# Thirteen filler matmuls ahead of the first products, the first attention's front ordered by batch half, and a comparison as a two-operand operation

## The chip, the cores and the metric

The kernel runs on one core of a Trainium2 chip. A core has TensorE (matmuls; PE in the profile, with PEld for its weight loads), VectorE (DVE), ScalarE (ACT), GpSimd (POOL) and SyncE (SP, which only issues transfers here). The metric is the device time of one execution in microseconds, as the median of several runs; lower is better.

## The reference

The kernel computes four layers on x, of 2 batches x 256 tokens x 128 features, all in float32, and each adds to x behind a scalar gate:

```python
x = x + tanh(g_xattn[0]) * L0_xattn(layernorm(x), ctx)    # 16 heads of 8; head h attends only to keys h, h+16, ...
x = x + tanh(g_ffn[0]) * L0_ffn(layernorm(x))             # 8 experts, each takes the 64 tokens with its best scores
x = x + tanh(g_xattn[1]) * L1_xattn(layernorm(x), ctx, ctx)  # 16 heads over all 512 context rows
x = x + tanh(g_ffn[1]) * L1_ffn(layernorm(x))             # 16 experts, one per token, plus a shared one
```

The change touches the first layer and one step of the second. In the first, a head sees one key in sixteen, so that the scores of all heads fit into one product of a token tile with the keys, if the keys are masked so that row d of key s is kept only where feature d belongs to head s mod 16:

```python
Q = (hidden @ Wq.T + bq);  K = (ctx @ Wk.T + bk);  V = (ctx @ Wv.T + bv)
attn = softmax(Q_h @ K_h[h::16].T * 8 ** -0.5);  out = (attn @ V_h[h::16]) @ Wo.T + bo
```

## The kernel before

The 512 tokens are four tiles of 128 (`NT`), two for each batch; the context is 2 x 512 rows, a half for each batch. Everything stays in SBUF, and PSUM is one tensor `bank` of eight banks. Each engine has its program written out by hand, and the engines meet only in semaphores: `then_inc` on the instruction that makes something, `wait_ge` ahead of the one that needs it. Nothing is reordered by a planner, so what is queued behind a waiting instruction waits too.

Transfers: SP issues x, the two halves of the context (`ctx`, `ctx_b`), constants and the later weights (lines 318 to 330). ScalarE's queue brings the identity and masks (`const`) and the weights `w0`, GpSimd's queue the small vectors (`small`), gates and rows.

The front of the first attention, by engine:

- VectorE takes statistics of the four x tiles (`ln_stats`), normalises them (`ln_apply`, line 1139, a tensor-scalar operation from SBUF to SBUF, 128 columns), copies the ones column of the values (`va0`, line 1150), masks the two halves of the keys from PSUM into `k0` (line 1155), and makes two broadcast columns `bvcol` (line 1162, two copies from SBUF to SBUF). Then come the four softmax tiles: a maximum (line 1175) and a subtraction (line 1176) each; `masked_v` (line 1168) takes the values of a half out of PSUM behind the third and the fourth.
- GpSimd computes the inverse deviations (lines 367, 371). Then it waits for the first masked keys, `k0_sb`, and fills three areas, one after the other, each awaited before the next: `va1` with zeros (4096 columns, line 395), its ones column (line 397), and the lower half of `kpack` with zeros (8192 columns, line 399). Behind these stand the gated bias and the residual tiles `xb`.
- TensorE transposes normalised tiles 0 and 1, multiplies the first context half into keys (`keys0`, lines 492 to 493), transposes tiles 2 and 3, and goes on to `queries0`, `keys0(1)`, `scores0`. It then waits for `bvcol_set` and for rows, adds the bias row, makes the value products (eight, bank 2 and 3), and goes on to the turned probabilities and the weighted sums `weighted0`.
- ScalarE copies the four turned tiles (line 978), then makes four query tiles `q0T` (line 984), then the exponentials.

A float32 product stands in the trace as two records, each a pass of its own.

In the second layer VectorE finds the 64th best score of each expert (`edge`), and compares all scores with it: `atleast` (line 1223, a tensor-scalar operation with `edge` as its scalar, 16 partitions x 256), and `gradeT` (line 1224, with two tensors). Meanwhile TensorE runs value products of the second attention, then `keep_running(28, 7)`, 28 products of zeros that nobody reads (line 602), and then transposes `gradeT`. `zeros_bf`, set by GpSimd, is the stationary operand of all such fillers.

Of the kernel before, what the change touches and what calls it, by code (L numbers as in the profile page):

```python
# [25 lines left out]
P = 128  # L26
D = 128
NB = 2
SQ = 256
SK = 512  # L30
T = NB * SQ
NT = T // P
KC = SK // P
H = 16
DH = D // H
# [9 lines left out]
HE = 2 * E0  # L45
HT = T // 2
# [26 lines left out]
V_BQ, V_BK, V_BV, V_LNW, V_LNB, V_BQ1, V_BK1, V_BV1 = range(8)  # L73
# [25 lines left out]
ALU = mybir.AluOpType  # L99
ACT = mybir.ActivationFunctionType  # L100
AX_X = mybir.AxisListType.X
F32 = mybir.dt.float32
BF16 = mybir.dt.bfloat16
# [3 lines left out]
def build(nc, x, small, consts, selq, onerows, gates, rows, ctxT, w0, w1, fc1T, fc2, b2, shGU, shD, gateup, down, kscr, qscr, out):  # L107
    with ExitStack() as ctx:
        def sb(name, shape, dt=F32):
            return ctx.enter_context(nc.sbuf_tensor(name, shape, dt))  # L110
# [4 lines left out]
        bank = ctx.enter_context(nc.psum_tensor("bank", [P, 8, 512], F32))  # L115
# [21 lines left out]
        def vec(n):  # L137
            return small_sb[:, C_VEC + n:C_VEC + n + 1]
# [19 lines left out]
        normedT = [sb(f"normedT{k}", [P, NT, P]) for k in range(2)] * 2  # L158
# [8 lines left out]
        selq_bf = sb("selq_bf", [P, 3, HPE, NROW], BF16)  # L167
        selq_up = sb("selq_up", [P, 3, HPE, NROW], BF16)
        iota_bf = sb("iota_bf", [P, CAP0], BF16)
        zeros_bf = sb("zeros_bf", [P, P], BF16)  # L170
        bvcol = sb("bvcol", [P, 2, P])
        bias = sb("bias", [P, 2, D])
        gbias = sb("gbias", [P, 2, D])
# [8 lines left out]
        def late_view(at, n, pattern, dt=F32, **k):  # L182
# [100 lines left out]
                                           "b2", "sh", "gu", "down")}  # L283

        S = {n: sem(n) for n in (
            "half_set", "vchain", "gchain", "tanh_done", "consts_bf", "bvcol_set", "k0_ps", "v0_ps", "k0_sb",
            "va0_sb", "bias0_ps", "bias0_sb", "xb0", "xb1", "nT0_ps", "nT0_sb", "q0_ps", "q0_sb", "sc0_ps",
            "shift0", "probs0_sb", "p0T_ps", "p0T_sb", "pv0_ps", "att0", "attT0_ps", "attT0_sb", "o0_ps", "nT1_ps",
            "nT1_sb", "lg0_ps", "sh0", "ex0", "score_sb", "scT_ps", "top_zero", "gradeT_sb", "grade_ps", "above_sb", "equal_sb",
# [64 lines left out]
        def _(pool):  # L354
# [1 line left out]
            pool.dma_start(gates_sb[:], gates).then_inc(L["gates"], 16)  # L356
            pool.dma_start(rows_sb[:], rows).then_inc(L["rows"], 16)
            pool.dma_start(b2_sb[:], b2).then_inc(L["b2"], 16)
            pool.memset(minus_half[:], -0.5).then_inc(S["half_set"], 1)
            pool.memset(zeros_bf[:], 0.0).then_inc(S["half_set"], 1)  # L360
            pool.memset(top[:], 0.0).then_inc(S["top_zero"], 1)
            pool.wait_ge(S["half_set"], 1)

            def ln_rstd(k, i):

# [4 lines left out]
                pool.wait_ge(S["gchain"], gc[0])  # L370
                pool.tensor_tensor(rstd[:, k, i:i + 2], rstd[:, k, i:i + 2], minus_half[:, i:i + 2], ALU.pow)\  # L371
                    .then_inc(LN_RS, 2)

            gc = [0]

            def link(ins):

                gc[0] += 1
                ins.then_inc(S["gchain"], 1)
                pool.wait_ge(S["gchain"], gc[0])  # L380

            def residual_bias(l, src):

# [91 lines left out]
        def _(pe):  # L475
            def mm(o, lhsT, rhs, start=True, stop=True, **k):
                return pe.matmul(o, lhsT, rhs, start=start, stop=stop, **k)  # L477
# [5 lines left out]
            def keep_running(n, at_bank):  # L483

                for _ in range(n):
                    mm(bank[:, at_bank, 0:T], zeros_bf[:], selq_bf[:].rearrange("p k h r -> p (k h r)")[:, 0:T])

            def normed0_turned(i):
                pe.wait_ge(LN_N, 0 * NT + i + 1)
# [2 lines left out]
            def keys0(b):  # L492
                mm(bank[:, b, :], w0_sb[:, 1, :], ctxT_sb[:, b * SK:(b + 1) * SK]).then_inc(S["k0_ps"], 1)

            def queries0(i):
                pe.wait_ge(S["nT0_sb"], i + 1)
                if i >= 2:
                    pe.wait_ge(S["q0_sb"], i - 1)
                mm(bank[:, 2 + i % 2, 0:P], w0_sb[:, 0, :], normedT[0][:, i, :]).then_inc(S["q0_ps"], 1)

            def scores0(i):
                pe.wait_ge(S["k0_sb"], i // 2 + 1)
                pe.wait_ge(S["q0_sb"], i + 1)
                mm(bank[:, 4 + i, :], q0T[:, i, :], k0[:, i // 2, :]).then_inc(S["sc0_ps"], 1)

            pe.wait_ge(L["const"], 16)
            normed0_turned(0)
            normed0_turned(1)
            pe.wait_ge(L["w0"], 16)
            pe.wait_ge(L["ctx"], 16)  # L510
            keys0(0)
            normed0_turned(2)
            normed0_turned(3)
            queries0(0)
            queries0(1)
            pe.wait_ge(L["ctx_b"], 16)
            keys0(1)
            scores0(0)
            scores0(1)
            queries0(2)  # L520
            queries0(3)
            scores0(2)
# [75 lines left out]
            mm(bank[:, 6, 0:D], bvcol[:, 1, :], w1_sb[:, 3, :], stop=False)  # L598
            mm(bank[:, 6, 0:D], const_sb[0:1, K_ONE:K_ONE + P], rows_sb[0:1, 1, :], start=False).then_inc(S["bias1_ps"], 1)
            pe.wait_ge(L["selq"], 16)  # L600
            pe.wait_ge(S["half_set"], 2)
            keep_running(28, 7)
            pe.wait_ge(S["gradeT_sb"], 1)
            pe.wait_ge(S["bias1_sb"], 1)
# [256 lines left out]
            def no_window(at_bank):  # L861

                for w, n in ((0, T), (1, WIDE - T)):
                    mm(bank[:, at_bank + w, 0:n], zeros_bf[:], selq_bf[:].rearrange("p k h r -> p (k h r)")[:, 0:n])

            def gate_up(e, at):
                for k, o in ((0, gate_ps), (1, up_ps)):
# [100 lines left out]
        def _(act):  # L968
# [5 lines left out]
            def copies(ps, sbs, dst, src):  # L974

                for i in range(NT):
                    act.wait_ge(S[ps], i + 1)
                    act.copy(dst(i), src(i)).then_inc(S[sbs], 1)  # L978

            act.wait_ge(L["small"], 16)  # L980
            copies("nT0_ps", "nT0_sb", lambda i: normedT[0][:, i, :], lambda i: bank[:, 4 + i, 0:P])
            for i in range(NT):
                act.wait_ge(S["q0_ps"], i + 1)
                act.activation(q0T[:, i, :], bank[:, 2 + i % 2, 0:P], ACT.Identity, bias=vec(V_BQ)).then_inc(S["q0_sb"], 1)
            for i in range(NT):
                act.wait_ge(S["shift0"], i + 1)
                act.activation(probs0[:, i, :], shifted[:, i, :], ACT.Exp, scale=SCALE).then_inc(S["probs0_sb"], 1)
# [136 lines left out]
        def _(dve):  # L1124
            chain = [0]

            def link(ins):

                chain[0] += 1
                ins.then_inc(S["vchain"], 1)  # L1130
                dve.wait_ge(S["vchain"], chain[0])
# [5 lines left out]
            def ln_apply(k, i):  # L1137
                dve.wait_ge(LN_RS, ln_done(k, i))
                dve.tensor_scalar(normed[k][:, i, :], ln_in[k][:, i, :], meanvar[:, k, i, 0:1], rstd[:, k, i:i + 1],  # L1139
                                  ALU.subtract, ALU.mult).then_inc(LN_N, 1)  # L1140

            dve.wait_ge(L["x"], 16)
            for i in range(NT):
                ln_stats(0, i, x_sb[:, i, :])
            for i in range(NT):
                ln_apply(0, i)
            dve.wait_ge(L["const"], 16)
            he = const_sb[:, K_HE:K_HE + H]
            hs = const_sb[:, K_HS:K_HS + H]
            dve.tensor_copy(va0[:, :, :, DH:DH + 1],  # L1150
                            hs.unsqueeze(1).unsqueeze(3).to_broadcast([P, NB * KC, H, 1]))
            dve.wait_ge(L["small"], 16)
            for b in range(NB):
                dve.wait_ge(S["k0_ps"], b + 1)
                dve.scalar_tensor_tensor(
                    out=k0[:, b, :].rearrange("p (j h) -> p j h", h=H),
                    in0=bank[:, b, :].rearrange("p (j h) -> p j h", h=H), scalar=vec(V_BK),
                    in1=he.unsqueeze(1).to_broadcast([P, SK // H, H]), op0=ALU.add, op1=ALU.mult)\
                    .then_inc(S["k0_sb"], 1)

            for l, v in ((0, V_BV), (1, V_BV1)):
                dve.tensor_copy(bvcol[:, l, :], vec(v).to_broadcast([P, P])).then_inc(S["bvcol_set"], 1)

# [56 lines left out]
            link(dve.stream_shuffle(other[:], top[:], [(p + E0) % HE if p < HE else p for p in range(32)]))  # L1220
            link(dve.tensor_tensor(pairmax[:], top[0:HE, :], other[0:HE, ::-1], ALU.max))
            link(dve.tensor_reduce(edge[:], pairmax[:], AX_X, ALU.min))
            link(dve.tensor_scalar(atleast[:], scoreT, edge[:], None, ALU.is_ge))
            dve.scalar_tensor_tensor(out=gradeT[:], in0=scoreT, scalar=edge[:], in1=atleast[:],
                                     op0=ALU.is_gt, op1=ALU.add).then_inc(S["gradeT_sb"], 1)
            dve.wait_ge(S["grade_ps"], 1)
# [292 lines left out]
```

## Time and profile before

| | before |
|---|---|
| median of 3 runs | 185.77 us (185.43 to 186.42) |
| the profiled execution's own time | 186.36 us |
| its span, first to last instruction | 184.5 us |
| mean granted clock of TensorE | 0.972 |
| busy: PE / DVE / ACT / POOL | 87% / 60% / 47% / 34% |

Busy shares are averages over stages. The page also follows the chain of work that ended last back from the last instruction. Where two steps of a helper share a line (477 and 481 are the matmul and the transpose of every stage), the tile names tell them apart: `w_sb` is `w0_sb` or `w1_sb`, `va` is `va0` or `va1`, `k` and `bvcol` are as in the code. A timeline row gives start, length, engine, line, operation, tiles and count; where operations of a row follow each other closely they are merged (x2, x4). A bracket tells how long the engine sat idle before, and who ended that. A row of a window (`39.50:40.00`) gives its length, then the busy time of PE, PEld, DVE, ACT and POOL, and last the granted clock as a share of full speed, the DMA share and GB/s.

### The profile page before, as it was taken

Reading aid. Unit: us, or ns where it says so; the run is one execution under the profiler, and the core shown is the slowest. Engines: PE = TensorE matmul, PEld = TensorE weight load, DVE = VectorE, ACT = ScalarE, POOL = GpSimd, SP = SyncE. Lnnn points to the kernel's source line nnn. Section 1 sums busy time; section 2 is a strip of 40 time slices with the busy share of each in tenths; the row PEclk is TensorE's granted clock in tenths of the full one; section 3 lists DMA queues with packets and bytes.
Section 4 is the critical chain, followed back from the end, with each engine's and each line's share of the span. In section 5 each row is a group of like instructions: output and inputs, shape, how many; then the busy total and the mean of one; then the engine's idle time right before and its main releaser. Section 6 shows DMA issues by size and latency. Waiting matters only on the chain.

```text
span 184.5 us, 3393 instructions
## 1 busy us (share of the span) xinstructions
PE 159.9 (87%) x1260; PEld 107.0 (58%) x1260; DVE 109.8 (60%) x300; ACT 85.9 (47%) x148; POOL 61.8 (34%) x91
## 2 busy tenths in 40 slices
PE   0599997699999999988999999989965876899994
PEld 0356883564589884754454444435434634499994
DVE  1557767796733475899988988970514695001032
ACT  2124537252046106548987787788820454301020
POOL 6489904986192722697000000000203342000000
PEclk9999999569999999999999999999999789999999
DMA  5999800005777590005200000000015000000002
GB/s 163 382 350 430 367 13 2 0 18 154 171 160 149 108 362 25 25 23 89 39 4 0 0 4 0 0 4 0 0 21 210 0 2 2 4 0 4 0 0 64
DMA packets 4294, 15.43 MB, mean 84 GB/s; under 512 B 948, under 2 KB 1844, under 8 KB 3492
## 3 DMA queue, kind: packets, MB, share of 16 engines
q1 hardware_dynamic: 2980, 11.66, 20.2%
q10 hardware_dynamic: 576, 2.44, 4.0%
q0 software_dynamic: 720, 1.09, 2.8%
q8 instruction: 12, 0.20, 0.4%
q14 instruction: 6, 0.05, 0.1%
HBM read 13.94 MB, written 1.25 MB: 82 GB/s over the span
## 4 chain that ended last, share of the span: by engine, by line
PE 74%; DVE 14%; issue 5%; POOL 2%; ACT 2%; DMA 2%; POOLq 0%
PE bank L477 69%; DVE mx L1326 6%; PE bank L481 5%; DVE stats L1134 2%; DMA x_sb<-in_x 2%; POOL rstd L371 2%; DVE normed L1139 1%; DVE meanvar L1135 1%; DVE res_b L1190 1%; POOL rstd L367 1%; PE bank L650 0%; ACT outT L1061 0%; DVE res_b L1292 0%; DVE kpack L1369 0%; ACT va L1100 0%
## 5 line engine op out<-in xcount | busy, mean ns | idle before, releaser
L1326 DVE TENSOR_REDUCE mx<-bank 128x1 f32<-128x512 f32 x64 | 41.7, 687 | 5.0 <-PE bank L477 4.5
L1067 ACT ACTIVATE arena<-bank 128x1024 f32<-128x1024 f32 x32 | 31.9, 1025 | 8.3 <-PE bank L477 7.8
L367 POOL TENSOR_SCALAR rstd<-meanvar 128x2 f32<-128x2 f32 x10 | 2.2, 223 | 65.4 <-DVE meanvar L1135 65.4
L477 PE MATMUL bank<-kpack,fc1T_sb 72*128 72x512 bf16 x64 | 22.7, 383 | 0.7 <-DVE mx L1326 0.5
L477 PE MATMUL bank<-fc1T_sb,kpack 104*128 104x256 bf16 x128 | 19.3, 272 | 0.1
L477 PE MATMUL bank<-arena,va 128*32 128x256 f32 x256 | 18.6, 387 | 0.5 <-ACT outT L1061 0.5
L477 PEld LDWEIGHTS bank<-fc1T_sb,kpack 104*128 104x128 bf16 x128 | 12.0, 97 | 6.4 <-issue 1.6
L477 PE MATMUL bank<-selq_bf,zeros_bf 128*128 128x512 bf16 (+1 forms) x57 | 13.4, 379 | 1.4 <-issue 1.4
L481 PE MATMUL bank<-const_sb,normed 128*128 128x128 f32 x16 | 4.5, 347 | 9.7 <-DVE normed L1139 9.5
L477 PEld LDWEIGHTS bank<-kpack,fc1T_sb 72*128 72x128 bf16 x64 | 6.1, 97 | 11.3 <-issue 5.2
L481 PEld LDWEIGHTS bank<-const_sb,normed 128*128 128x128 f32 x16 | 2.3, 156 | 14.1 <-issue 7.1
L477 PE MATMUL bank<-normedT,shGU_sb 128*128 128x256 f32 (+1 forms) x24 | 9.3, 536 | 1.3 <-issue 1.3
L477 PEld LDWEIGHTS bank<-arena,va 128*32 128x32 f32 x256 | 6.2, 108 | 6.8 <-issue 4.6
L477 PEld LDWEIGHTS bank<-selq_bf,zeros_bf 128*128 128x128 bf16 x57 | 5.5, 100 | 7.0 <-issue 2.1
L477 PE MATMUL bank<-kpack,arena 128*128 128x128 f32 (+1 forms) x72 | 8.6, 278 | 0.0
L1408 DVE TENSOR_TENSOR kpack<-bank,kpack 128x768 f32<-128x768 f32 x1 | 1.0, 957 | 12.7 <-ACT kpack L1115 12.7
L1075 ACT CAST fc1T_sb<-bank 8x1024 bf16<-8x1024 f32 x8 | 8.0, 1005 | 0.9 <-PE bank L477 0.8
L477 PEld LDWEIGHTS bank<-kpack,arena 128*128 128x128 f32 x72 | 8.2, 192 | 0.3 <-issue 0.2
L477 PE MATMUL bank<-kpack,fc_sb 128*128 x64 | 7.4, 276 | 1.0 <-ACT kpack L1113 1.0
L477 PEld LDWEIGHTS bank<-kpack,fc_sb 128*128 128x128 f32 x64 | 7.2, 192 | 1.2 <-issue 1.2
L978 ACT COPY normedT<-bank 128x128 f32<-128x128 f32 x12 | 2.9, 266 | 10.4 <-PE bank L481 10.3
L371 POOL TENSOR_TENSOR rstd<-rstd,minus_half 128x2 f32<-128x2 f32 x10 | 7.1, 713 | 1.5
(223 smaller groups left out, 314.8 us busy)
## 6 DMA issues: line engine op xcount, KB each, us to landing
kpack<-k_parts SPq DMA_DIRECT2D x3, 768.0 KB
fc1T_sb<-in_fc1T SPq DMA_DIRECT2D x1, 2048.0 KB, 11.8
fc_sb<-in_fc SPq DMA_DIRECT2D x1, 2048.0 KB, 16.1
fc_sb<-in_gateup ACTq DMA_DIRECT2D x2, 1024.0 KB, 6.0
arena<-in_down SPq DMA_DIRECT2D x1, 1024.0 KB, 6.4
k_parts<-arena SPq DMA_DIRECT2D x8, 96.0 KB, 2.2
fc1T_sb<-q_rows POOLq DMA_DIRECT2D x9, 64.0 KB, 2.8
ctxT_sb<-in_ctxT SPq DMA_DIRECT2D x2, 256.0 KB, 4.7
```

The lines of the kernel that those rows point to most:

```text
L367: pool.tensor_scalar(rstd[:, k, i:i + 2].unsqueeze(2), meanvar[:, k, i:i + 2, 1:2], EPS, None, ALU.add)\
L371: pool.tensor_tensor(rstd[:, k, i:i + 2], rstd[:, k, i:i + 2], minus_half[:, i:i + 2], ALU.pow)\
L477: return pe.matmul(o, lhsT, rhs, start=start, stop=stop, **k)
L481: return pe.transpose(o, src, ident[0:n, 0:n])
L978: act.copy(dst(i), src(i)).then_inc(S[sbs], 1)
L1067: act.activation(probs1[:, n % (2 * GH), :, :], bank[:, 2 + 2 * (n % 2):4 + 2 * (n % 2), :], ACT.Exp, scale=SCALE)\
L1075: act.copy(qpack[MROW:KROWS, b, g * GH:(g + 1) * GH, :], bank[MROW:KROWS, r, 0:SQ].unsqueeze(1).to_broadcast([2 * GH, GH, SQ]))\
L1134: link(dve.bn_stats(stats[:, k, i, :], src))
L1135: dve.bn_aggr(meanvar[:, k, i, :], stats[:, k, i, :]).then_inc(LN_MV, 1)
L1139: dve.tensor_scalar(normed[k][:, i, :], ln_in[k][:, i, :], meanvar[:, k, i, 0:1], rstd[:, k, i:i + 1], ALU.subtract, ALU.mult).then_inc(LN ...
L1190: dve.scalar_tensor_tensor(out=res[0][:, i, :], in0=bank[:, 4 + i, 0:D], scalar=tanhg[:, 0:1], in1=xb_sb[:, i, :], op0=ALU.mult, op1=ALU.a ...
L1326: dve.tensor_reduce(mx1[:, b * 2 + qt, g * GH + j:g * GH + j + 1], bank[:, r, :], AX_X, ALU.max)\
```

## The change

Three edits.

*Fillers.* VectorE first sets a new tile `quiet` (128 x 512, bfloat16) to zero, ahead of its wait for x, and `zeros_bf` becomes its first 128 columns. TensorE waits for that alone and issues 13 products of 512 columns out of `quiet` into bank 7, which nobody reads, before its first wait for data. GpSimd's memset of `zeros_bf` and the semaphore `half_set`, and TensorE's wait on it ahead of the 28 fillers, are gone; GpSimd's `link` helper is defined earlier and now orders the memset of `minus_half`.

*Order by halves.* TensorE, ScalarE and VectorE now do everything of batch half 0 (tiles 0 and 1, context half 0) as far as the scores before half 1. On TensorE the first keys product stands ahead of the transposes and ahead of the wait for `const`. On VectorE the masking of the first keys stands between the normalisations of tiles 0, 1 and those of tiles 2, 3, and the `va0` copy behind those. The `bvcol` copies stay behind the masking of the second keys.

*Comparison.* `atleast` becomes a tensor-tensor operation, with `edge` broadcast along the row as its second operand.

```diff
-        zeros_bf = sb("zeros_bf", [P, P], BF16)
+        quiet = sb("quiet", [P, T], BF16)
+        zeros_bf = quiet[:, 0:P]
@@ gpsimd
-            pool.memset(minus_half[:], -0.5).then_inc(S["half_set"], 1)
-            pool.memset(zeros_bf[:], 0.0).then_inc(S["half_set"], 1)
+            link(pool.memset(minus_half[:], -0.5))
             pool.memset(top[:], 0.0).then_inc(S["top_zero"], 1)
-            pool.wait_ge(S["half_set"], 1)
@@ tensor
+            pe.wait_ge(S["quiet_set"], 1)
+            for _ in range(13):
+                mm(bank[:, 7, 0:T], zeros_bf, quiet[:])
+            pe.wait_ge(L["w0"], 16)
+            pe.wait_ge(L["ctx"], 16)
+            keys0(0)
             pe.wait_ge(L["const"], 16)
             normed0_turned(0)
             normed0_turned(1)
-            pe.wait_ge(L["w0"], 16)
-            pe.wait_ge(L["ctx"], 16)
-            keys0(0)
+            queries0(0)
+            queries0(1)
+            scores0(0)
+            scores0(1)
+            pe.wait_ge(L["ctx_b"], 16)
+            keys0(1)
             normed0_turned(2)
             normed0_turned(3)
-            queries0(0)
-            queries0(1)
-            pe.wait_ge(L["ctx_b"], 16)
-            keys0(1)
-            scores0(0)
-            scores0(1)
             queries0(2)
             queries0(3)
...
-            pe.wait_ge(S["half_set"], 2)
             keep_running(28, 7)
@@ scalar
-            copies("nT0_ps", "nT0_sb", lambda i: normedT[0][:, i, :], lambda i: bank[:, 4 + i, 0:P])
-            for i in range(NT):
-                act.wait_ge(S["q0_ps"], i + 1)
-                act.activation(q0T[:, i, :], bank[:, 2 + i % 2, 0:P], ACT.Identity, bias=vec(V_BQ)).then_inc(S["q0_sb"], 1)
+            for half in ((0, 1), (2, 3)):
+                for i in half:
+                    act.wait_ge(S["nT0_ps"], i + 1)
+                    act.copy(normedT[0][:, i, :], bank[:, 4 + i, 0:P]).then_inc(S["nT0_sb"], 1)
+                for i in half:
+                    act.wait_ge(S["q0_ps"], i + 1)
+                    act.activation(q0T[:, i, :], bank[:, 2 + i % 2, 0:P], ACT.Identity, bias=vec(V_BQ)).then_inc(S["q0_sb"], 1)
@@ vector
+            dve.memset(quiet[:], 0.0).then_inc(S["quiet_set"], 1)
             dve.wait_ge(L["x"], 16)
             for i in range(NT):
                 ln_stats(0, i, x_sb[:, i, :])
-            for i in range(NT):
-                ln_apply(0, i)
-            dve.wait_ge(L["const"], 16)
...
+            for i in (0, 1):
+                ln_apply(0, i)
+            dve.wait_ge(L["const"], 16)
+            dve.wait_ge(L["small"], 16)
+            masked_keys(0)
+            for i in (2, 3):
+                ln_apply(0, i)
+            dve.tensor_copy(va0[:, :, :, DH:DH + 1],
+                            hs.unsqueeze(1).unsqueeze(3).to_broadcast([P, NB * KC, H, 1]))
+            masked_keys(1)
             for l, v in ((0, V_BV), (1, V_BV1)):
                 dve.tensor_copy(bvcol[:, l, :], vec(v).to_broadcast([P, P])).then_inc(S["bvcol_set"], 1)
...
-            link(dve.tensor_scalar(atleast[:], scoreT, edge[:], None, ALU.is_ge))
+            link(dve.tensor_tensor(atleast[:], scoreT, edge[:].to_broadcast([HE, HT]), ALU.is_ge))
```

## Rows read from the trace of the kernel before

**Rows 1.** The page: granted clock in 40 slices, and the chain by engine.
```profile
PEclk9999999569999999999999999999999789999999
...
PE 74%; DVE 14%; issue 5%; POOL 2%; ACT 2%; DMA 2%; POOLq 0%
```

**Rows 2.** Timeline of 0 to 30 us, all engines: start, length, engine, line.
```profile
0.73 0.39 SPq L318 DMA_DIRECT2D x_sb<-in_x  x1
...
6.49 0.66 PE L481 MATMUL bank<-const_sb,normed 128*128 128x128 f32 x2 [6.49 <-DVE normed L1139]
...
7.58 0.28 DVE L1150 COPY va<-const_sb 128x128 f32<-128x128 f32 x1
...
9.78 3.51 POOL L395 MEMSET va<- 128x4096 f32 x1 [2.75 <-DVE k L1155]
...
11.88 0.75 DVE L1155 SCALAR_TENSOR_TENSOR k<-bank,small_sb,const_sb 128x512 f32<-128x512 f32 x1 [2.16 <-PE bank L477]
...
13.36 0.67 DVE L1175 TENSOR_REDUCE mx<-bank 128x16 f32<-128x512 f32 x1
...
13.74 6.92 POOL L399 MEMSET kpack<- 64x8192 f32 x1
...
17.26 2.05 PE L477 MATMUL bank<-w_sb,ctxT_sb 128*128 128x128 f32 x16
...
18.46 0.88 DVE L1168 TENSOR_TENSOR va<-bank,const_sb 128x128 f32<-128x128 f32 x4 [1.06 <-PE bank L477]
...
20.43 1.25 PE L477 MATMUL bank<-va,arena 128*128 128x144 f32 x8 [0.24 <-ACT arena L993]
```

**Rows 3.** Passes of the score products: count, ns min/median/max, first and last start.
```profile
L477 PE MATMUL bank<-k,q0T x8: 592/592/1051, 11.6 to 16.1; 128*128 128x512 f32 x8
```

**Rows 4.** Timeline of VectorE in short windows: normalisations, then each bvcol copy.
```profile
5.99 0.61 DVE L1139 TENSOR_SCALAR normed<-x_sb,meanvar,rstd 128x128 f32<-128x128 f32 x2 [0.54 <-POOL rstd L371]
...
12.55 0.82 DVE L1162 COPY bvcol<-small_sb 128x128 f32<-128x128 f32 x1
...
12.68 0.76 DVE L1162 COPY bvcol<-small_sb 128x128 f32<-128x128 f32 x1
```

**Rows 5.** Timelines of GpSimd and VectorE, and line 1391 (ns min/median/max).
```profile
43.18 1.06 DVE L1223 TENSOR_SCALAR atleast<-q0T,edge 16x256 f32<-16x256 f32 x1
...
142.12 0.67 POOL L460 IOTA kpack<- 128x640 f32 x1
...
142.20 0.74 DVE L1139 TENSOR_SCALAR normed<-res_b,meanvar,rstd 128x128 f32<-128x128 f32 x2 [1.20 <-POOL rstd L371]
...
142.74 0.34 POOL L462 MEMSET kpack<- 128x128 f32 x1
...
150.10 1.40 POOL L469 TENSOR_TENSOR va<-va 128x512 f32<-128x512 f32 x1 [1.82 <-ACT va L1103]
...
152.23 1.15 POOL L471 TENSOR_TENSOR va<-va 128x512 bf16<-128x512 f32 x1 [0.73 <-ACT va L1106]
...
L1391 DVE TENSOR_SCALAR kpack<-kpack,place x4: 544/548/1447, 149.0 to 150.4; 128x640 bf16<-128x640 f32 x4
```

**Rows 6.** TensorE and VectorE near the 28 fillers; clock of one half microsecond.
```profile
34.59 3.62 PE L477 MATMUL bank<-w_sb,ctxT_sb 128*128 128x128 f32 x16
...
39.29 0.86 PE L477 MATMUL bank<-selq_bf,zeros_bf 128*128 128x512 bf16 x2
...
39.50:40.00 0.50, 0.50 (x3) 0.16 (x2) 0.47 (x3) 0.16 (x1) 0.50 (x2) 0.65 0.00 0
...
44.28 0.47 DVE L1224 SCALAR_TENSOR_TENSOR gradeT<-q0T,edge,atleast 16x256 f32<-16x256 f32 x1
...
45.69 0.29 PE L481 MATMUL bank<-const_sb,gradeT 16*128 16x16 f32 x2
```

**Rows 7.** Transfers: size and median us from issue to landing (issued at 1.18 and 1.64).
```profile
ctxT_sb<-in_ctxT SPq DMA_DIRECT2D x2, 256.0 KB, 4.7
```

More of the change, by code:

```diff
@@ L285, in build @@
         S = {n: sem(n) for n in (
-            "half_set", "vchain", "gchain", "tanh_done", "consts_bf", "bvcol_set", "k0_ps", "v0_ps", "k0_sb",
+            "quiet_set", "vchain", "gchain", "tanh_done", "consts_bf", "bvcol_set", "k0_ps", "v0_ps", "k0_sb",
             "va0_sb", "bias0_ps", "bias0_sb", "xb0", "xb1", "nT0_ps", "nT0_sb", "q0_ps", "q0_sb", "sc0_ps",
@@ L358, in _, with link @@
             pool.dma_start(b2_sb[:], b2).then_inc(L["b2"], 16)
-            pool.memset(minus_half[:], -0.5).then_inc(S["half_set"], 1)
-            pool.memset(zeros_bf[:], 0.0).then_inc(S["half_set"], 1)
+            gc = [0]
+            def link(ins):
+                gc[0] += 1
+                ins.then_inc(S["gchain"], 1)
+                pool.wait_ge(S["gchain"], gc[0])
+            link(pool.memset(minus_half[:], -0.5))
             pool.memset(top[:], 0.0).then_inc(S["top_zero"], 1)
-            pool.wait_ge(S["half_set"], 1)
             def ln_rstd(k, i):
@@ L372, in ln_rstd @@
                     .then_inc(LN_RS, 2)
[L374 to L380, printed above, removed]
             def residual_bias(l, src):
@@ L485, in keep_running @@
                 for _ in range(n):
-                    mm(bank[:, at_bank, 0:T], zeros_bf[:], selq_bf[:].rearrange("p k h r -> p (k h r)")[:, 0:T])
+                    mm(bank[:, at_bank, 0:T], zeros_bf, selq_bf[:].rearrange("p k h r -> p (k h r)")[:, 0:T])
             def normed0_turned(i):
@@ L863, in no_window @@
                 for w, n in ((0, T), (1, WIDE - T)):
-                    mm(bank[:, at_bank + w, 0:n], zeros_bf[:], selq_bf[:].rearrange("p k h r -> p (k h r)")[:, 0:n])
+                    mm(bank[:, at_bank + w, 0:n], zeros_bf, selq_bf[:].rearrange("p k h r -> p (k h r)")[:, 0:n])
             def gate_up(e, at):
@@ L1144, in _, with masked_keys @@
                 ln_stats(0, i, x_sb[:, i, :])
-            for i in range(NT):
-                ln_apply(0, i)
-            dve.wait_ge(L["const"], 16)
             he = const_sb[:, K_HE:K_HE + H]
             hs = const_sb[:, K_HS:K_HS + H]
[L1150 to L1153, printed above, removed]
+            def masked_keys(b):
                 dve.wait_ge(S["k0_ps"], b + 1)
```

## Prediction, made before the changed kernel was run

> **What bounds the kernel now.** I read the page first, for its chain of work [rows 1]: TensorE carries 74% of it, but that is an average, and what an edit is worth has to be read from its own stage. So the next view is the timeline of the first 28 us [rows 2]. TensorE begins at 6.49 us. It is busy from there, yet slow: one pass of a 128x512 f32 product takes 1.05 us up to about 12.5 and 0.59 us afterwards [rows 3], which are the two levels of its clock, 1.2 and 2.4 GHz. (The page's granted clock says full speed in both places [rows 1]; only the durations show it here.) From 13.36 VectorE works through the softmax tiles, each a maximum (0.67 us) and a subtraction, and from 20.43 TensorE runs nearly back to back through the weighted sums. Behind 20.43 all follows in a fixed order, so what the front gains or loses up to the first weighted sum passes on to the end, apart from what the clock does further down.
>
> The second thing to see is what holds VectorE at 12.55. The two bvcol copies take 0.82 and 0.76 us and end at 13.37 and 13.44 [rows 4], though a copy of the same 128x128 size takes 0.28 [rows 2]. GpSimd's memset of va1 runs from 9.78 to 13.29 [rows 2]; both copies end right behind it. Two more places look alike [rows 5]. The pair of normalisations at 142.20 takes 0.74 us, not 0.61 as at 5.99 [rows 4], and ends just behind GpSimd's iota (142.12 + 0.67). The last selection of line 1391 takes 1.45 us against 0.55 for the least of the four, and ends 0.35 us behind GpSimd's subtraction (150.10 + 1.40). So copies and tensor-scalar operations from SBUF to SBUF, normalisations among them, are held while GpSimd works on a large tile. Operations that read PSUM are not: masking the second half of the keys took 0.75 us at 11.88, in the middle of the memset [rows 2].
>
> **The change part by part.** *Fillers.* VectorE can set quiet from 0.73 us, when the queues start [rows 2]. The nearest rows for the memset are the 0.28 us copy and the 0.67 us maximum over 512 columns [rows 2]; I take 0.45, so that fillers start at about 1.2. One costs 0.43 us at the low clock (two run in 0.86 [rows 6]) and half of that at the high one. Thirteen end at 6.8 if all are slow, at 4.0 if all are fast. The first context half and w0 land about 1.18 + 4.7 = 5.9 [rows 7], so the first keys product, which now waits for nothing else, runs between 5.9 and 6.8: the fillers cost at most 0.9 us of readiness. The clock rose 6.0 us (6.49 to 12.5) and 5.3 us (34.59 to 39.85, where the granted clock of the half microsecond is 0.65) after dense work began [rows 3, 6]; from 1.2 on that is 6.5 to 7.2, so keys run fast or nearly so.
>
> *Front by halves.* Keys take two passes, 0.43 + 0.59 = 1.02 us fast, their masking 0.75. Masking of half 0 ended just before 9.78, where it released the memset of va1. Now it ends at T0 = 7.7 to 8.6, say 8.2 (9.5 if keys are still slow), and releases that memset at once. But two normalisations now stand right behind this masking on VectorE; before, they were over when the va0 copy began at 7.58. VectorE starts an operation 0.08 us before the last one ends (bvcol at 12.55, masking until 12.63), and the second of a pair 0.26 us after the first (0.61 - 0.35). So they start at T0-0.08 and T0+0.18, and the second at least meets the memset and waits for its end, E = T0 + 3.6 = 11.8. That GpSimd gets in between two queued VectorE operations is what line 1391 shows: its subtraction, issued at 150.10 during one selection, took 0.25 us more than the like one at 152.23, and then held the next selection [rows 5].
>
> Queued behind on VectorE: the va0 copy (0.28, until 12.1), the masking of half 1 (0.75, until 12.8; its keys are there at 11.6: q0T at 8.9, two score products of 0.85, keys 1.02), then, from 12.7, the bvcol copies. GpSimd goes on meanwhile: its kpack memset starts 0.45 us behind the end of va1's (13.74 after 13.29), at 12.25, for 6.92 us. Before, bvcol slipped in between the two; now it comes half a microsecond too late and is held until 12.25 + 6.92 = 19.2, done at 19.3 against 13.44. Behind bvcol stand all four softmax tiles on VectorE, and on TensorE, which waits for bvcol_set, the bias row and the value products.
>
> To the first weighted sum two paths compete. VectorE: three tiles take 4.04 us (13.36 to 17.40, where its idle 1.06 us before 18.46 begin), masking of V 0.88 [rows 2]: 19.2 + 4.04 + 0.88 = 24.1, that is 3.7 us later than 20.43, the least loss. TensorE: bias 0.73 and values 2.05 us fast, 1.4 and 3.6 slow [rows 2, 6]; then 1.2 us (from 17.26 + 2.0 to 20.43) for transposes and their copy, up to 1.7 slow. It has been idle since about 15 by then. All slow, 19.3 + 1.4 + 3.6 + 1.7 = 26.0, a loss of 5.6. I take 4.9, nearer the slow end: after the thin stretch before 34.59 the clock was low, but a pause of four microseconds need not do it. T0 moves this by 0.4 either way.
>
> *Other waits.* On ScalarE the copies of tiles 2 and 3 now stand behind q0T of half 0; those tiles come from the late normalisations anyway. kpack's memset ends 1.5 us earlier than before (19.2, 20.66), so GpSimd's xb tiles and SP's transfer of ones behind kpack_zero come no later. The memset of zeros_bf and the waits on half_set that go stood in stretches where GpSimd waited for statistics and TensorE ran fillers: nothing.
>
> *Comparison.* With two operands it costs 0.47 us by the nearest row (line 1224, the same tile, two SBUF inputs [rows 6]) and at most the present 1.06 if it is held [rows 5]: 0 to 0.6 us of VectorE. But gradeT is ready at 44.28 + 0.47 = 44.75 and the transposes that use it start at 45.69, behind the 28 fillers [rows 6]. With that cover of 0.94 us it is worth nothing. Had the value products of 34.59 run at the high clock (2.05 instead of 3.6 us), VectorE would be last and the edit would count in full.
> The Trainium skill ("SBUF — State Buffer", Who interferes with whom) says that a VectorE operation with two SBUF inputs contends with a GpSimd one that reads SBUF; by it the new form would be held at line 1223 like the old and give nothing even then, so that the chance kept below for it would go. No row here shows that form beside a large GpSimd operation.
>
> **The sum.** Against the profiled execution (span 184.5, time 186.36 us): +4.9, so 191.3. That execution lies 0.6 us above the median of 185.77, so the median goes to 190.7. This case alone reaches from 189.0 (3.7 less 0.4) to 191.8 (5.6 plus 0.4).
>
> **Rivals.** *A, the pair gets through (the other side).* VectorE keeps its turn over both normalisations. For it: the held pair at 142.20 was out by 142.94 though GpSimd's next memset had been issued at 142.74 [rows 5]; against it, line 1391. The memset of va1 then runs from T0+0.5 to 12.1, kpack's from 12.6. Masking of half 1 ends at 12.4, and bvcol, issued at 12.3, goes first. First maximum at 12.8 (0.6 earlier), the second half's scores done at 14.9 instead of 16.7, values at 17.6 (19.3), first weighted sum at 18.8: 1.6 us gained, between 1.1 and 2.4. Median 184.1. It decides from where bvcol is issued before kpack's memset, and it has 0.3 us for that.
> The same section of the skill has the ports given to one side for a whole instruction, to whoever issues first; by that rule the turn isn't kept over a pair and A falls, which gives 190.7. The row at 142.20 doesn't decide it, since the memset behind it is short.
>
> *B, only the normalisation is held.* bvcol still comes ahead of kpack's memset, because GpSimd needs 0.5 us longer between its memsets than the 0.45 of [rows 2]. First maximum at 13.2, values at 17.8: 1.4 us gained, 184.4.
>
> *C, the front doesn't count.* Nothing is held and the clock further down takes the gain back: within 0.9 us of now. The stage from 20.43 on has no slack that speaks for it.
>
> **How the numbers follow.** Forecast, bvcol held by kpack's memset: 0.63. A 0.22, B 0.11 (in a few hundredths of these the comparison counts too), C 0.04. A measurement of this kernel tells 0.5%, 0.93 us, from no change. So faster 0.33, same 0.04, slower 0.63. The forecast is the likeliest case, 190.7, with its own 189.0 to 191.8. As a third of the chance lies on the other side, the range goes from 183.4 (A less 0.7) to 191.8.
>
> **What would show it.** Right: the bvcol copies last some 6 us and end within 0.2 us of kpack's memset; a normalisation of tile 2 or 3 lasts about 3.5 us; the first maximum is past 18.5. Wrong: normalisations of 0.35 us beside the memset, or bvcol done before 13.5. Fillers: thirteen, ending by 6.8, and keys at 0.59 us a pass. Comparison: gradeT earlier, its transposes behind the fillers as late as before.

## The result

The changed kernel takes 191.5 us (median of 4 runs, 191.29 to 191.72), the kernel before in the same comparison 185.6 us (184.38 to 186.42). The ratio is 1.0333, with a 95% interval of 1.0292 to 1.0374. The case of the forecast (bvcol held by the memset of kpack) came true. Its 190.7 us was 0.8 us too low, near the upper end of its own range (191.8).

| | before | after |
|---|---|---|
| profiled execution: time, span | 186.36, 184.5 us | 191.72, 189.9 us |
| mean granted clock | 0.972 | 0.955 |
| first maximum on VectorE | 13.36 us | 19.07 us |
| first weighted sum on TensorE | 20.43 us | 25.71 us |
| from there to the end of the span | 164.1 us | 164.2 us |

The page of the changed kernel, the lines that answer to [rows 1]: a dip has come into the granted clock in the fourth and fifth slice of 4.7 us (8, then 5), and in the chain that ended last `bvcol` is new, with 3%, and `normed` has gone from 1% to 3%. VectorE made both late.

```profile
PEclk9998599957999999999999999999999879999999
...
PE 69%; DVE 20%; issue 5%; DMA 3%; POOL 2%; ACT 1%; ACTq 0%; POOLq 0%; DVEq 0%
PE bank L476 64%; DVE mx L1337 6%; PE bank L480 4%; DVE bvcol L1173 3%; DVE normed L1143 3%; DMA w_sb<-in_w 3%; DVE stats L1138 2%; POOL rstd L378 1%; DVE meanvar L1139 1%; DVE res_b L1201 1%; DVE k L1156 1%; PE bank L651 0%; ACT outT L1065 0%; POOL rstd L374 0%; DVE res_b L1303 0%
```

The timeline of the changed kernel from 0 to 26 us, all engines (columns as in [rows 2]):

```profile
0.85 0.27 DVE L1146 MEMSET quiet<- 128x256 uint32 x1 [0.85 <-PEq L1518]
...
1.18 4.44 PE L476 MATMUL bank<-quiet 128*128 128x512 bf16 x13 [1.18 <-DVE quiet L1146]
...
5.98 1.12 PE L476 MATMUL bank<-ctxT_sb,w_sb 128*128 128x512 f32 x2 [0.37 <-DMA w_sb<-in_w]
...
7.25 0.75 DVE L1156 SCALAR_TENSOR_TENSOR k<-bank,small_sb,const_sb 128x512 f32<-128x512 f32 x1 [0.40 <-PE bank L476]
...
7.92 3.80 DVE L1143 TENSOR_SCALAR normed<-x_sb,meanvar,rstd 128x128 f32<-128x128 f32 x2
8.06 3.51 POOL L394 MEMSET va<- 128x4096 f32 x1 [0.78 <-DVE k L1156]
...
11.64 0.49 DVE L1169 COPY va<-const_sb 128x128 f32<-128x128 f32 x1
...
11.77 0.74 DVE L1156 SCALAR_TENSOR_TENSOR k<-bank,small_sb,const_sb 128x512 f32<-128x512 f32 x1
12.05 6.95 POOL L398 MEMSET kpack<- 64x8192 f32 x1
...
12.43 6.71 DVE L1173 COPY bvcol<-small_sb 128x128 f32<-128x128 f32 x2
...
19.07 0.67 DVE L1186 TENSOR_REDUCE mx<-bank 128x16 f32<-128x512 f32 x1
...
19.20 0.80 PE L476 MATMUL bank<-w_sb,bvcol 128*128 128x128 f32 x2 [3.82 <-DVE bvcol L1173]
...
20.65 3.78 PE L476 MATMUL bank<-w_sb,ctxT_sb 128*128 128x128 f32 x16
...
23.03 0.87 DVE L1179 TENSOR_TENSOR va<-bank,const_sb 128x128 f32<-128x128 f32 x4
...
25.71 0.51 PE L476 MATMUL bank<-va,arena 128*128 128x144 f32 x2 [0.24 <-ACT arena L997]
```

Read it from the memsets. The one of `va1` ends at 11.57; the pair of normalisations that began at 7.92 ends at 11.72. The one of `kpack` ends at 19.00, the pair of `bvcol` copies at 19.14. In between GpSimd began `kpack` at 12.05 and VectorE came to `bvcol` at 12.43, 0.38 us too late. TensorE sat idle for 3.82 us, for `bvcol` alone. The windows around that idle time (length, busy PE, PEld, DVE, ACT, POOL, granted clock, DMA share, GB/s) show the granted clock fall to half in it (0.82, then 0.50), and rise again in the half microsecond from 24.50, more than 5 us after work resumed at 19.20. So the value products ran at 1.2 GHz (3.78 us; 2.05 in [rows 2]):

```profile
17.50:18.00 0.50, 0.00 (x0) 0.00 (x0) 0.50 (x2) 0.00 (x0) 0.50 (x1) 0.82 0.85 360
18.00:18.50 0.50, 0.00 (x0) 0.00 (x0) 0.50 (x2) 0.00 (x0) 0.50 (x1) 0.50 1.00 426
24.00:24.50 0.50, 0.50 (x5) 0.50 (x4) 0.50 (x1) 0.00 (x0) 0.00 (x0) 0.50 0.00 0
24.50:25.00 0.50, 0.50 (x6) 0.50 (x5) 0.47 (x1) 0.00 (x0) 0.00 (x0) 0.85 0.00 0
```

The second place, the comparison (timeline of 34 to 52 us), answers to [rows 5, 6]. The new form takes 1.19 us beside GpSimd's subtraction, and the transposes of `gradeT` still stand behind the fillers, 0.81 us after it is ready at 50.17.

```profile
44.98 6.07 PE L476 MATMUL bank<-selq_bf,quiet 128*128 128x512 bf16 x27 [0.33 <-issue]
...
48.23 1.16 POOL L420 TENSOR_TENSOR arena<-arena 128x512 f32<-128x512 f32 x1 [0.73 <-ACT arena L1029]
48.48 1.19 DVE L1234 TENSOR_TENSOR atleast<-q0T,edge 16x256 f32<-16x256 f32 x1
...
49.70 0.47 DVE L1235 SCALAR_TENSOR_TENSOR gradeT<-q0T,edge,atleast 16x256 f32<-16x256 f32 x1
...
50.98 0.29 PE L480 MATMUL bank<-const_sb,gradeT 16*128 16x16 f32 x2
```

Some executions take over 1.5% longer than the fastest of their kernel: in the table below, medians are over all executions, ratios leave such ones out, and the profiled execution of e1 was one of them (187.78 us), so that its rest is not given.

### The profile page after: what moved, and what is told of

Read it like the earlier page. It is cut to its first block, busy times and chain, and to the rows that moved or that the text cites. A ratio compares the mean times of both kernels' runs of the same rounds, so it can differ in the third digit from the quotient of the medians.

```text
span 189.9 us, 3412 instructions
## 1 busy us (share of the span) xinstructions
PE 164.5 (87%) x1268; PEld 109.4 (58%) x1273; DVE 118.9 (63%) x301; ACT 85.8 (45%) x148; POOL 61.8 (33%) x90
## 4 chain that ended last, share of the span: by engine, by line
PE 69%; DVE 20%; issue 5%; DMA 3%; POOL 2%; ACT 1%; ACTq 0%; POOLq 0%; DVEq 0%
PE bank L476 64%; DVE mx L1337 6%; PE bank L480 4%; DVE bvcol L1173 3%; DVE normed L1143 3%; DMA w_sb<-in_w 3%; DVE stats L1138 2%; POOL rstd L378 1%; DVE meanvar L1139 1%; DVE res_b L1201 1%; DVE k L1156 1%; PE bank L651 0%; ACT outT L1065 0%; POOL rstd L374 0%; DVE res_b L1303 0%
## 5 line engine op out<-in xcount | busy, mean ns | idle before, releaser
L476 PE MATMUL bank<-fc1T_sb,kpack 104*128 104x256 bf16 x128 | 19.3, 272 | 0.1
L476 PE MATMUL bank<-selq_bf,quiet 128*128 128x512 bf16 (+1 forms) x52 | 12.1, 374 | 2.3 <-issue 2.1
L476 PEld LDWEIGHTS bank<-selq_bf,quiet 128*128 128x128 bf16 x57 | 5.5, 100 | 7.2 <-issue 2.2
L476 PEld LDWEIGHTS bank<-normedT,shGU_sb 128*128 128x128 f32 x24 | 5.3, 237 | 3.8 <-issue 3.1
L476 PE MATMUL bank<-w_sb,ctxT_sb 128*128 128x128 f32 x32 | 7.4, 426 | 0.0
L476 PE MATMUL bank<-arena,fc1T_sb 128*128 128x64 f32 x64 | 7.3, 275 | 0.0
```

## The experiments

All are given in one table. "Rest" is the span of the profiled execution less the start of its first weighted sum. Kernels of a group ran together with the kernel before, whose median there stands behind the group's name. Its executions spread over some 4 us (183.97 to 187.96), so differences below half a per cent are not read.

| kernel | first maximum | first weighted sum | rest | median (n) | ratio to before, 95% |
|---|---|---|---|---|---|
| before / after | 13.36 / 19.07 | 20.43 / 25.71 | 164.1 / 164.2 | 185.6 / 191.5 (4) | 1.0333 [1.0292, 1.0374] |
| *group 1 (before: 185.53)* | | | | | |
| e1_pool_behind_bvcol | 13.02 | 19.23 | | 185.18 (12) | 0.9981 [0.9934, 1.0028] |
| e2_bvcol_first | 12.37 | 18.95 | 163.6 | 184.58 (10) | 0.9977 [0.9939, 1.0015] |
| e3_bvcol_up_pool_behind | 12.08 | 18.55 | 163.9 | 184.37 (10) | 0.9974 [0.9939, 1.0010] |
| e6_kpack_in_two | 16.36 | 21.34 | 163.5 | 186.67 (4) | 1.0115 [1.0056, 1.0173] |
| *group 2 (before: 184.96)* | | | | | |
| e10_bvcol_two_operands | 12.91 | 19.19 | 163.9 | 184.92 (10) | 1.0002 [0.9972, 1.0032] |
| e4_fillers_alone | 12.63 | 17.82 | 164.1 | 182.99 (4) | 0.9877 [0.9822, 0.9932] |
| e5_order_no_fillers | 14.86 | 21.34 | 163.9 | 187.27 (10) | 1.0052 [0.9999, 1.0105] |
| e8_old_comparison | 12.51 | 18.99 | 163.3 | 184.14 (12) | 0.9957 [0.9926, 0.9988] |
| *group 3 (before: 186.06)* | | | | | |
| e11_fillers_bvcol_first | 10.43 | 17.71 | 163.8 | 183.29 (4) | 0.9844 [0.9793, 0.9896] |
| e12_keys_ahead_too | 10.82 | 18.09 | 164.3 | 183.48 (4) | 0.9851 [0.9797, 0.9906] |
| e7_cmp_alone | 13.42 | 20.46 | 164.3 | 185.92 (12) | 0.9996 [0.9961, 1.0031] |

The rest is 163.3 to 164.3 us in all these traces: the first weighted sum tells the time of a profiled execution to within a microsecond.

### Is it the hold of bvcol, and what decides it?

**e1**: GpSimd starts its memsets behind `bvcol` instead of behind the first masked keys.

```diff
-            pool.wait_ge(S["k0_sb"], 1)
+            pool.wait_ge(S["bvcol_set"], 2)
```

> The changed kernel, with one wait replaced: GpSimd begins its three memsets behind bvcol_set (2) instead of behind the first masked keys. Theory H (a copy or normalisation of VectorE from SBUF to SBUF is held while GpSimd fills a large tile, and the bvcol copies are what costs): nothing is held, bvcol is done at 12.6, the first maximum starts at 12.5 (19.07 in the changed kernel), the first weighted sum at 18.6 (25.71), and the time falls by about 7 us to 184.4. The residual tiles of GpSimd may then be late by a few tenths. Rival R (the order by halves or the clock costs by itself, the long copies only stand beside it): the copies may be short, but the time stays above 190.

Nothing is held, and the first weighted sum comes 6.5 us earlier than in the changed kernel. The memsets themselves now begin at 13.16:

```profile
8.48 0.59 DVE L1143 TENSOR_SCALAR normed<-x_sb,meanvar,rstd 128x128 f32<-128x128 f32 x2
...
12.75 0.35 DVE L1173 COPY bvcol<-small_sb 128x128 f32<-128x128 f32 x2
...
13.16 3.51 POOL L394 MEMSET va<- 128x4096 f32 x1 [6.17 <-DVE bvcol L1173]
```

**e2**: the changed kernel with the two copies ahead of the first masking.

```diff
+            for l, v in ((0, V_BV), (1, V_BV1)):
+                dve.tensor_copy(bvcol[:, l, :], vec(v).to_broadcast([P, P])).then_inc(S["bvcol_set"], 1)
             masked_keys(0)
...
             masked_keys(1)
-            for l, v in ((0, V_BV), (1, V_BV1)):
-                dve.tensor_copy(bvcol[:, l, :], vec(v).to_broadcast([P, P])).then_inc(S["bvcol_set"], 1)
```

> The changed kernel, with the bvcol copies moved ahead of the masking of the first keys; GpSimd as it was. H: the copies take 0.3 us; the normalisations of tiles 2 and 3 are still held for 3.6 us by the memset of va1, but they cost little, since the second keys are ready only at 11.5; first maximum at 12.5, first weighted sum at 18.8, 184.5 us. If the held normalisations are a large part of the loss instead, the time stays 2 us or more above the kernel with GpSimd moved. R: above 190.

The copies are free; the normalisations are held as before, and that costs next to nothing:

```profile
6.70 0.35 DVE L1167 COPY bvcol<-small_sb 128x128 f32<-128x128 f32 x2
...
7.75 3.80 DVE L1143 TENSOR_SCALAR normed<-x_sb,meanvar,rstd 128x128 f32<-128x128 f32 x2
...
7.90 3.51 POOL L394 MEMSET va<- 128x4096 f32 x1 [0.68 <-DVE k L1156]
...
11.54 0.44 PE L480 MATMUL bank<-const_sb,normed 128*128 128x128 f32 x2
```

The transposes of tiles 2 and 3, which need these normalisations, start at 11.54 and have no bracket, so TensorE did not sit idle before them: in this order it is at the second keys until then.

**e3**: GpSimd waits as in e1, and the copies stand right behind the normalisations of tiles 2 and 3.

> The changed kernel, with the bvcol copies right behind the normalisations of tiles 2 and 3, and GpSimd's memsets behind bvcol_set (2), so that nothing of VectorE meets them. H: normalisations 0.35 us each at 8 to 8.6, bvcol done at 9.0, memsets from 9.0 to 20.0, first maximum at 12.4, first weighted sum at 18.6, 184.0 us, the lowest of the four. R: above 190.

Against e2 the first weighted sum comes 0.40 us earlier, but the first normalisations of this execution did too, by 0.25 us (5.92 against 6.17). That leaves 0.15 us for 3.5 us of held normalisations, less than such executions differ by.

**e10**: the changed kernel, with `bvcol` at its late place but made by an operation of two SBUF operands (times a tile of ones, whose landing it waits for).

```diff
-                dve.tensor_copy(bvcol[:, l, :], vec(v).to_broadcast([P, P])).then_inc(S["bvcol_set"], 1)
+                dve.tensor_tensor(bvcol[:, l, :], vec(v).to_broadcast([P, P]), const_sb[:, K_ONE:K_ONE + P],
+                                  ALU.mult).then_inc(S["bvcol_set"], 1)
```

> The changed kernel with the two bvcol copies as products of two SBUF operands (the column times a tile of ones) at the same place, still behind the masking of the second keys and so inside the kpack memset. If the hold depends on the form (copies and tensor-scalar operations need what GpSimd holds, a two-operand operation only meets a GpSimd operation that reads SBUF, and a memset doesn't): 0.29 us each, done at 12.8, first weighted sum at 18.9, 184.6 us. If everything from SBUF to SBUF is held: they end at 19.1 and the time stays 191.5.

This is the sharpest of them, for nothing changes its place. The pair runs through in 0.48 us inside the memset of `kpack`:

```profile
8.00 3.80 DVE L1143 TENSOR_SCALAR normed<-x_sb,meanvar,rstd 128x128 f32<-128x128 f32 x2
8.14 3.51 POOL L394 MEMSET va<- 128x4096 f32 x1 [0.92 <-DVE k L1156]
...
12.12 6.95 POOL L398 MEMSET kpack<- 64x8192 f32 x1
...
12.51 0.48 DVE L1174 TENSOR_TENSOR bvcol<-small_sb,const_sb 128x128 f32<-128x128 f32 x2
12.91 0.68 DVE L1188 TENSOR_REDUCE mx<-bank 128x16 f32<-128x512 f32 x1
```

Against the changed kernel the first weighted sum comes 6.52 us earlier. The hold depends on the form of VectorE's operation and on what GpSimd does: a copy is held by a memset, the product of two tiles is not; the two-operand comparison, on the other hand, is held beside GpSimd's subtraction, which reads SBUF (1.19 us above, 0.41 in e1 when the subtractions were over). The Trainium skill ("SBUF — State Buffer", Who interferes with whom) has it so: a two-input operation contends with a GpSimd instruction that reads SBUF and not with one that only writes it. The traces agree on both halves.

**e6**: the memset of `kpack` as two of 4096 columns, to see if the hold goes with the length of one instruction.

> The changed kernel, with the kpack memset in two halves of 4096 columns, the second behind the first. H, with the hold lasting one instruction: bvcol gets in between the halves, at 15.5 instead of 19.1, the clock doesn't fall in the shorter pause, first weighted sum at 20.8, 186.6 us. If the hold lasted as long as GpSimd has any work: bvcol ends at 19.1 and the time stays 191.5. R: 191.5 too.

```profile
12.76 3.53 POOL L399 MEMSET kpack<- 64x4096 f32 x1
...
13.14 3.30 DVE L1175 COPY bvcol<-small_sb 128x128 f32<-128x128 f32 x2
...
16.34 3.54 POOL L400 MEMSET kpack<- 64x4096 f32 x1
...
17.32 2.05 PE L478 MATMUL bank<-w_sb,ctxT_sb 128*128 128x128 f32 x16
...
21.34 1.22 PE L478 MATMUL bank<-va,arena 128*128 128x144 f32 x8 [0.89 <-DVE va L1181]
```

The copies wait for one instruction of GpSimd, not for its queue: they end at 16.44, within 0.15 us of the first half's end (16.29), though the second half is issued then. (`bvcol` was expected at 15.5; the whole front of this execution is 0.7 us later than that of the changed kernel, the keys having waited 0.93 us for `w0`.) TensorE's pause is short, 0.40 us, and the value products are fast (2.05 us). This also prices the clock in the changed kernel: here the first weighted sum comes 4.90 us after `bvcol` is done (21.34 - 16.44). By that the changed kernel's would come at 19.14 + 4.90 = 24.04; it came at 25.71. So 1.67 us of its loss are the slow clock behind the pause. The two traces bear this out: in e6 the first weighted sum waited for VectorE's values, in the changed kernel these were ready at 23.90 (the row at 23.03), and TensorE, at its slow products, came to it 1.8 us later.

### What each edit is worth without the hold

**e4**: the kernel before with `quiet` and the 13 fillers, the order and the comparison of before.

> The kernel before with the first part of the change alone: quiet, 13 fillers, and the wait for quiet_set; order and comparison as before. If the low clock at the front is what the fillers remove: keys and scores at 0.59 us a pass from 6.9 us on, first maximum at 12.5 (bvcol still meets the memset of va1, which now ends near 12.4), first weighted sum at 18.0 (20.43), 183.9 us, at or below the kernel with bvcol and GpSimd moved. If the front's pace isn't set by the clock: 185.5, as before.

```profile
9.05 3.51 POOL L394 MEMSET va<- 128x4096 f32 x1 [1.74 <-DVE k L1157]
...
10.36 2.35 DVE L1164 COPY bvcol<-small_sb 128x128 f32<-128x128 f32 x2
...
12.63 0.67 DVE L1177 TENSOR_REDUCE mx<-bank 128x16 f32<-128x512 f32 x1
```

The first weighted sum comes 2.61 us earlier, a little more than expected (18.0 us), and the time falls by 1.2% (0.9822 to 0.9932, an interval that lies below 1). The fillers alone make a faster kernel than before. `bvcol` is held here too, by the memset of `va1`, for 2.3 us.

**e5**: e3 without the 13 fillers.

> The kernel with bvcol up and GpSimd behind it (nothing held), without the 13 fillers: what the order by halves brings alone. Low clock until 9 to 12.5 us: keys 1.9 us, scores 3.4 us of it, first maximum at 14, first weighted sum at 20.0, 185.4 us, 1 us above the same kernel with fillers. If the order carries the gain and the fillers none: 184.4.

The first weighted sum falls back by 2.79 us (18.55 to 21.34), so the fillers are worth about the same in either order. It was expected at 20.0, and the time at 185.4. With them gone the new order is 0.9 us behind the old one even with nothing held (20.43).

**e8**: e3 with the comparison of before. **e7**: the kernel before with the new comparison alone.

> The kernel with bvcol up and GpSimd behind it, with the comparison of before (tensor-scalar). In that kernel the two-operand form took 1.20 us beside GpSimd's subtraction and VectorE was last by 0.46 us. If both forms are held until the subtraction ends: the old form takes 1.06 us, the time is the same within 0.2 us. If only the old form is held in full and the two-operand one partly, it gets slower by up to 0.4 us.

> The kernel before with the two-operand comparison alone. Theory (it is held by GpSimd's subtraction like the old form, and is covered by the 28 fillers either way): the comparison takes 1.0 to 1.2 us as the old 1.06, the transposes of gradeT start at 45.7, time as before, 185.4 within 0.3. Rival (the new form isn't held, 0.47 us): gradeT 0.6 us earlier, time the same because of the fillers. Rival (the comparison counts): 184.8.

In e7 the new form takes 1.19 us beside GpSimd's subtraction, the old 1.06 in [rows 5], and the transposes of `gradeT` start at 45.71 (45.69 in [rows 6]). In e8 the old form took 1.28, in e3 the new 1.20. Only in e1, where GpSimd was through with its large subtractions, did the new form take 0.41. By the ratio of e7, 0.9996 (0.9961 to 1.0031), the comparison is worth nothing.

e8 against e4 is also nearly the order alone, since both have the old comparison and ran together: 184.14 against 182.99 us, first weighted sum 18.99 against 17.82. (They differ in the hold of `bvcol` too, 2.3 us in e4 and none in e8; e11 below shows that this is worth 0.11 us.)

**e11**: e4 with the `bvcol` copies ahead of both maskings. **e12**: e11 with the first keys product ahead of the first transposes.

> The kernel before with the 13 fillers ahead, and with the bvcol copies moved ahead of both maskings of the keys, so that no memset holds them. With the fillers alone the copies lasted 2.3 us and the first maximum came at 12.63 us, the value products at 14.66, the first weighted sum at 17.82. Theory (TensorE sets this stage, not the hold): the copies take 0.22 us each, the first maximum comes at 10.5, but the bias rows still stand behind the last scores (13.9) and the transposes of the probabilities behind the value products (16.55), so the first weighted sum stays at 17.8 and the time at 182.9. Rival (every held bvcol costs its own length): the first weighted sum comes 2.1 us earlier, at 15.7, and the time is 180.9.

> As the kernel with fillers and early bvcol copies, and the first keys product ahead of the first two transposes on TensorE, as the change has it. Keys start at 6.0 us, when w0 has landed, instead of 7.1. Theory (the normalisations, 6.3 to 7.9 us, set the queries and thereby the scores): masking of half 0 comes 0.3 us earlier, scores stay at 9.2 to 9.5, the second half's scores at 11.9 to 12.1; time 182.7, within 0.3 of the kernel without this move. Rival (the keys are the bound): all comes 1 us earlier, 181.8.

```profile
7.88 0.35 DVE L1156 COPY bvcol<-small_sb 128x128 f32<-128x128 f32 x2
...
10.43 0.69 DVE L1176 TENSOR_REDUCE mx<-bank 128x16 f32<-128x512 f32 x1
...
12.03 1.95 PE L476 MATMUL bank<-k,q0T 128*128 128x512 f32 x4 [0.33 <-ACT q0T L985]
...
17.71 1.25 PE L476 MATMUL bank<-va,arena 128*128 128x144 f32 x8 [0.24 <-ACT arena L994]
```

These are rows of e11. The first maximum comes 2.20 us earlier than in e4, the first weighted sum 0.11: a held `bvcol` costs only what outlasts TensorE's queue, for the bias row and the value products stand behind the last scores anyway. e12 didn't test what it was for, keys at 6.0 us. Its fillers ended at 6.91, its keys began at 6.70, not at 6.0, because all thirteen ran at the low clock:

```profile
1.18 5.73 PE L476 MATMUL bank<-quiet 128*128 128x512 bf16 x13 [1.18 <-DVE quiet L1143]
6.70 0.70 PE L476 MATMUL bank<-ctxT_sb,w_sb 128*128 128x512 f32 x1
```

The fastest are e4, e11 and e12, by 1.2%, 1.6% and 1.5% against the kernel before; which of the three is the best their intervals don't tell.

**Why the order by halves costs.** Rows of e3, in which nothing is held:

```profile
7.52 0.71 PE L476 MATMUL bank<-normedT,w_sb 128*128 128x128 f32 x4 [0.54 <-ACT normedT L985]
...
8.56 1.96 PE L476 MATMUL bank<-k,q0T 128*128 128x512 f32 x4 [0.33 <-ACT q0T L988]
...
11.41 0.75 DVE L1156 SCALAR_TENSOR_TENSOR k<-bank,small_sb,const_sb 128x512 f32<-128x512 f32 x1 [2.78 <-PE bank L476]
11.83 0.71 PE L476 MATMUL bank<-normedT,w_sb 128*128 128x128 f32 x4 [0.25 <-ACT normedT L985]
...
12.08 0.68 DVE L1186 TENSOR_REDUCE mx<-bank 128x16 f32<-128x512 f32 x1
...
12.87 1.96 PE L476 MATMUL bank<-k,q0T 128*128 128x512 f32 x4 [0.33 <-ACT q0T L988]
```

The scores of half 0 start at 8.56, in e11 at 9.37. But VectorE can't use them: its masking of half 1 stands ahead of the first maximum and waits (2.78 us idle) for the second keys, which TensorE now does behind those scores. So the first maximum comes at 12.08, in e11 at 10.43. That takes the gain away, but it isn't the loss: e4 and e11 show that 2.20 us at the first maximum are worth 0.11. The loss is on TensorE. The scores of half 1 start at 12.87, in e11 at 12.03, which is the 0.84 us by which the first weighted sum comes later (18.55, 17.71), although e3 began its first real product 1.01 us sooner (5.64, 6.65). On the way TensorE waits four times for ScalarE, 1.45 us in all (the brackets above); in e11 once, 0.33 us, for there both keys products and the transposes of tiles 2 and 3 stand between the steps that e3 waits in. No run takes these waits out and keeps the order, so how much of the 0.84 us is theirs is not shown.

## Why the prediction was right, step by step

The loss of 5.28 us at the first weighted sum falls into steps between kernels, each with its own run: before 20.43; fillers added 17.82 (e4); `bvcol` freed 17.71 (e11); order by halves 18.55 (e3, nothing held); `bvcol` back at its place and the normalisations held 19.19 (e10); `bvcol` held 25.71. e3 and e8 have the same front and stand at 18.55 and 18.99, so a step of this row is good to some 0.4 us; those of the fillers, 2.61, of the order, 0.84 here and 1.17 between e4 and e8, and of the hold, 6.52, are beyond it. (e3 differs from e11 also in the form of the comparison, which stands further down, and in when GpSimd begins its memsets, 8.50 and 8.95.)

- *Where the time is read* (behind 20.43 all follows in a fixed order): right, by the column "rest".
- *Fillers' end*, 4.0 to 6.8: they ended at 5.62. The first keys then waited 0.37 us for `w0`, and ran fast, in 1.12 us. The memset of `quiet` took 0.27 us, not 0.45: it is written as 256 words. The clock rose about 3.0 us after the first filler, where I had 5.3 to 6.0; in e12 it rose no earlier than I had it. (Only the durations show it: the weight loads of the fillers stand 0.43 us apart up to 4.13 us, and the last five take 0.98 us; the granted clock of these windows reads 1.00 throughout.)
- *T0*, 8.2: 8.00. *End of the first hold*, 11.8: 11.57 for the memset, 11.72 for the pair. The second normalisation was to be held "at least"; both were (3.73 and 3.55 us in this trace, and likewise in e2, e6 and e10).
- *VectorE's queue behind it*, `bvcol` from 12.7 against a memset from 12.25: 12.43 against 12.05, a margin of 0.38 us instead of 0.45. The `va0` copy, which I had at 0.28, took 0.49, beside the short memset.
- *End of `bvcol`*, 19.3: 19.14.
- *The two paths to the first weighted sum*, 24.1 if fast and 26.0 if slow: 25.71, and 24.04 for the fast one by e6. I took 4.9 us of loss, it was 5.28: the clock fell at 17.5 to 18.0 and did not rise before 24.5, so the path of the slow end decided, 0.3 us short of its 26.0. This is the one term of the sum that was mis-sized, by 0.4 us. The other 0.4 us by which the median of 191.5 lies above the forecast come from the step to it: I put the median 0.6 us under the profiled execution, as in the kernel before, and it lies 0.2 us under it (191.72).
- *Comparison*, nothing: right. Its length was 0.41 free and 1.19 held. The rule of the Trainium skill ("SBUF — State Buffer", Who interferes with whom) on two-input operations, weighed in the prediction, was right: the hold made the new form no shorter than the old (1.19 and 1.06 us). The cover of 0.94 us was 0.81. In e2, e3 and e6 it is gone (TensorE waited 0.46 us for `gradeT` in e3); the two forms being alike, nothing came of that.
- *The rivals.* None of them came about. Case B's conditions are those of e10 (normalisations held, `bvcol` not). It had 1.4 us of gain; the trace of e10 has 1.24, its time 1.0002 of before (0.9972 to 1.0032). Its mechanism was no more than a sum of two parts that I had not split: fillers that give 2.6 us and an order that takes 0.8 of them back.

One thing stays open. The traces of e2, e3 and e10 show 1.2 to 1.9 us won at the first weighted sum, the ratios only 0 to 0.3%. Most executions of the kernel before lie between 184 and 186.5 us and the profiled one (186.36) is at the upper end, so part of what these traces win may be only that; where its faster executions win their 2 us no trace here shows. It bears on the worth of the fillers too, 2.61 us in the traces and 2.0 in the medians (184.96, 182.99). The spread itself differs: kernels without the fillers spread over 2.4 to 4.1 us (the kernel before in each group, e7, e5), four with them and ten or more executions over 1.0 to 1.6 (e2, e3, e8, e10); e1, with five of twelve near 188, is the exception. So the uneven part may be the cold start that the fillers cover, but no run shows that.

## What to carry to other kernels

A copy or a normalisation from SBUF to SBUF that is queued on VectorE just behind a large GpSimd memset takes as long as the memset (here 3.8 and 6.7 us for a pair): count the margin between the two issues, and move the small operation ahead, give it a two-operand form (this helped beside a memset, not beside a GpSimd operation that reads SBUF), or let GpSimd wait for it. When an order is changed so that one half is through sooner, look at what stands ahead of its consumer in that engine's own queue (here the other half's masking, so that the early scores were used no sooner), and at the work that used to fill the waits between two engines (here TensorE waited four times for ScalarE instead of once). Test the parts of a change apart: thirteen fillers alone were worth 1.2%, and stood in a change that cost 3.3%.

## What the runs showed of the hardware that was not expected

- VectorE's normalisation is held although its record starts before the memset's (7.92 and 8.06 us; 7.75 and 7.90 in e2; 8.00 and 8.14 in e10), so the starts of two records don't tell who gets through.
- The same 13 fillers took 4.44, 5.10 and 5.73 us in the traces of the changed kernel, e11 and e12: a product costs 0.21 us more at the low clock (0.43 against half of it), so e12 had six more of them there than the changed kernel, and its clock rose some 6 x 0.43 = 2.6 us later, though the work ahead is the same. What decides it no run here shows, with one traced execution of each.
